# Second expert mixture scatters its results; feature attention spreads VectorE's small operations and takes four strips at once in its last units

## What is computed

```python
def _moe(x, Wg, W1, W3, W2):                      # layer 5, HIDDEN = 704, TOP_K = 2
    gate_weights = jax.nn.softmax(jnp.einsum('bsd,de->bse', x, Wg), axis=-1)
    topk_w, topk_idx = jax.lax.top_k(gate_weights, TOP_K)
    topk_w = topk_w / jnp.sum(topk_w, axis=-1, keepdims=True)
    ...
        y = jnp.einsum('bsh,hd->bsd', jax.nn.silu(x @ W1[e]) * (x @ W3[e]), W2[e])
        out = out + combine[..., e:e + 1] * y

def _L3_xattn_ref(q, k, v):                       # layer 6: b = 16, d = 64, m = n = 256
    qh = q.reshape(b * 8, 8, m); kh = k.reshape(b * 8, 8, n); vh = v.reshape(b * 8, 8, n)
    sm = jax.nn.softmax(jnp.einsum('bdm,bdn->bmn', qh, kh) / sqrt(8), axis=-1)
    ret = jnp.einsum('bmn,bcn->bcm', sm, vh)
```

## Time and profile before

| | us |
|---|---|
| median of three runs (lowest, highest) | 1216.42 (1215.36, 1218.13) |
| the profiled execution, its own time | 1219.71 |
| its span, first to last instruction | 1217.9 |
| busy in the span: PE, DVE, ACT, POOL | 1068.7, 577.4, 370.0, 258.0 |
| second mixture, first gather of tokens to last addition to X | 658.57 to 884.97 |
| feature attention, first score matmul to last addition to X | 888.52 to 1065.50 |

### The profile page before, as it was taken

The page is one execution under the profiler, slowest core; times in us unless marked ns, Lnnn a source line. Parts: engine busy times, 40 slices in busy tenths (PEclk is TensorE's granted clock), DMA queues, the critical chain, the costliest instruction groups (busy, mean ns, idle before and its releaser), DMA issues.

```text
span 1217.9 us, 18073 instructions
## 1 busy us (share of the span) xinstructions
PE 1068.7 (88%) x6946; PEld 713.4 (59%) x6946; DVE 577.4 (47%) x1304; ACT 370.0 (30%) x691; POOL 258.0 (21%) x332
## 2 busy tenths in 40 slices
PE   5877999979999999978774999999179999889989
PEld 4665578746767677667663777777133333243457
DVE  6976412244343343355474221221266777248692
ACT  3641123232221221204210222221015555526560
POOL 4212332420000000003521111100452433011350
PEclk9995989989999999989986999999659999978999
DMA  9002023211010010065043102110230000010000
GB/s 269 24 2 95 17 71 86 79 31 49 18 36 28 25 36 5 10 211 216 2 168 109 31 27 104 35 35 18 74 148 1 1 1 1 1 69 1 0 9 26
DMA packets 36059, 66.11 MB, mean 54 GB/s; under 512 B 4456, under 2 KB 26824, under 8 KB 34440
## 3 DMA queue, kind: packets, MB, share of 16 engines
q1 hardware_dynamic: 25608, 48.70, 11.9%
q0 software_dynamic: 3744, 10.23, 3.1%
q10 hardware_dynamic: 6624, 6.03, 1.4%
HBM read 54.72 MB, written 10.22 MB: 53 GB/s over the span
## 4 chain that ended last, share of the span: by engine, by line
PE 74%; DVE 17%; issue 3%; ACT 3%; DMA 2%; POOL 2%; SPq 0%; DVEq 0%; ACTq 0%
PE bank L344 22%; PE bank L1132 12%; PE bank L1156 7%; PE bank L1413 5%; PE bank L2069 4%; PE bank L2087 3%; PE bank L1423 3%; PE bank L2108 3%; PE bank L2497 2%; PE bank L1145 2%; DVE big L1959 2%; PE bank L1398 2%; PE bank L1388 1%; PE bank L2121 1%; PE bank L2503 1%
## 5 line engine op out<-in xcount | busy, mean ns | idle before, releaser
L1132 PE MATMUL bank<-big 128*128 x552 | 155.5, 426 | 3.6 <-ACT big L1006 1.7
L344 PE MATMUL bank<-XNT,big 128*128 128x512 f32 x296 | 143.4, 636 | 4.5 <-DVE big L2246 2.8
L1132 PEld LDWEIGHTS bank<-big 128*128 128x128 f32 x552 | 98.0, 194 | 50.5 <-issue 12.1
L2069 PE MATMUL bank<-big,xs 32*128 32x512 f32 x256 | 94.2, 781 | 36.5 <-DVE xs L271 30.5
L265 POOL TENSOR_TENSOR rstd<-ve,half 128x1 f32<-128x1 f32 x64 | 38.7, 605 | 366.9 <-DVE ve L259 366.5
L1959 DVE TENSOR_REDUCE big<-bank 128x2 f32<-128x512 f32 x128 | 81.9, 685 | 39.6 <-PE bank L2069 39.2
L344 PEld LDWEIGHTS bank<-XNT,big 128*128 128x128 f32 x296 | 57.9, 203 | 72.1 <-issue 64.0
L1156 PE MATMUL bank<-big 128*128 (+1 forms) x368 | 87.2, 380 | 1.1 <-ACT big L1021 1.1
L2021 ACT ACTIVATE big<-bank 128x1024 f32<-128x1024 f32 x64 | 65.5, 1024 | 52.4 <-PE bank L2087 52.3
L950 DVE TENSOR_TENSOR big<-big,bank 128x704 f32<-128x704 f32 x23 | 20.4, 889 | 124.7 <-ACT big L1014 124.7
L2087 PE MATMUL bank<-big 32*128 32x512 f32 x256 | 78.3, 690 | 0.2
(11 more groups left out here) (344 smaller groups left out, 1785.5 us busy)
## 6 DMA issues: line engine op xcount, KB each, us to landing
big<-m_gu SPq DMA_DIRECT2D x8, 1408.0 KB
big<-a_qkv SPq DMA_DIRECT2D x16, 384.0 KB, 3.5
big<-m_d SPq DMA_DIRECT2D x8, 768.0 KB
yg<-big ACTq DMA_DIRECT2D x46, 128.0 KB
big<-m_gu SPq DMA_DIRECT2D x8, 352.0 KB
big<-a_o SPq DMA_DIRECT2D x16, 128.0 KB, 2.1
big<-f_keys SPq DMA_DIRECT2D x1, 2048.0 KB, 9.2
big<-p_gu SPq DMA_DIRECT2D x1, 2048.0 KB, 7.8
```

Source lines behind the costliest of these rows:

```text
L344: ins = e.matmul(out, a, b, start=start and n == 0, stop=stop and n == len(pairs) - 1)
L1132: ins = e.matmul(out, xgT[s % 2][:, kb, :], WB[:, bass.ds(at[s] + (kb * 2 * F + c * chunk), chunk)], start=kb == 0, stop=kb == KB - 1)
L2069: e.matmul(bank[:, step_bank(step), :], k.xs[t % 2][q, b * P:(b + 1) * P], cm[t % 2][q, 2 * jp:2 * jp + 2].rearrange("p j n -> p (j n)"), ...
```

## The change

The second mixture. The index that each slot carries is now the place of its result in `yg`: 128 + 1024 times the choice + the token (`token_at`, one more index table, so `CONST` is 13), and 0 for padding. `xn` is stored twice, with 128 rows of padding ahead, so that the same index gathers the tokens. Each result tile is scattered by POOL with an indirect DMA (`deliver`), where ScalarE's queue stored it. The two results of a token then lie at fixed rows, and SP loads them with plain DMAs, one per row tile into four buffers (`sp_last`, which `program` issues after the next layer's `sp_first`). The first mixture keeps its way.

Feature attention. 5 units (`FRONT`) instead of 6 stand ahead of the first transposed strips, and two follow them in the first round. VectorE's list is cut in halves: two maxima, one small operation, two maxima, one small operation; the reciprocal is two halves of 128 columns. From unit 26 (`LAST`) on, where no scores are left, the transposed strips use three pairs of banks in turn, both pairs are issued one after the other, then both value products of the unit before; the turned maxima and the sorted result move to bank 6.

```diff
@@ -780,19 +784,27 @@
     xg, ya = ring[:, 0:RING], ring[:, RING:2 * RING]
+    pairs = ring.rearrange("p (n q) d -> p n q d", q=2)
     gw = k.gates[:, shared_expert * 1]
     g = k.dram
-    xn_d, yg_d = g["xn"], g["yg"]
+    if shared_expert:
+        xn_d, yg_d = g["xn"][0:T], g["yg"]
+    else:
+        xn_d, yg_d = g["xn"], g["yg"][0:2 * T + P]
+        to_xn = xn_d[P:].rearrange("(c t p) d -> t p c d", p=P, t=NT)
+        from_yg = yg_d[P:].rearrange("(c t p) d -> t p c d", p=P, t=NT)
     if k.moe_at is None:
...
     S, start = k.moe, dict(k.moe_at)
-    ends = dict(gate_ld=16 * (1 + 4 * shared_expert), wts=16 * 2 * E, xn_st=16 * NT, lg_ps=NT, mx=1, ex=1, mk=1, cnt=1,
+    ends = dict(gate_ld=16 * (1 + 4 * shared_expert), wts=16 * 2 * E, xn_st=16 * (NT + 1 - LAG), lg_ps=NT, mx=1, ex=1, mk=1, cnt=1,
                 hot=2, inv_ps=1, inv_sb=1, inv_t=1, inv=1, eid=1, xgt_ps=TILES, xgt_sb=TILES, gu_ps=TILES, hs=TILES, h_sb=TILES,
-                ht_ps=TILES, ht_act=TILES, ht_dve=TILES * (NB > 4), y_ps=TILES, y_sb=TILES, ga0=16 * NT, ga1=16 * NT,
+                ht_ps=TILES, ht_act=TILES, ht_dve=TILES * (NB > 4), y_ps=TILES, y_sb=TILES, ga0=16 * NT * LAG, ga1=16 * NT * LAG,
                 sh_ps=6, sh_s=6, sh_u=6, sh_h=6, shy_ps=NT, shy=NT)
     ends.update({f"xg{q}": 16 * len(range(q, TILES, RING)) for q in range(RING)})
-    ends.update({f"y_st{q}": 16 * len(range(q, TILES, YS)) for q in range(YS)})
+    for q in range(YS):
+        ends[f"y_st{q}"], ends[f"dv{q}"] = [16 * len(range(q, TILES, YS)) * here for here in (LAG, 1 - LAG)]
+    ends.update({f"back{n}": 32 * (1 - LAG) for n in range(4)})
     k.moe_at = {n: start[n] + ends[n] for n in MOE_SEMS}
@@ -827,7 +839,20 @@
             e.wait_ge(k.ln_out, at0 + t + 1)
-            tell(e.dma_start(xn_d[t * P:(t + 1) * P, :], XN[:, t]), "xn_st", 16)
+            if shared_expert:
+                tell(e.dma_start(xn_d[t * P:(t + 1) * P, :], XN[:, t]), "xn_st", 16)
+            else:
+                tell(e.dma_start(to_xn[t], bc(XN[:, t], 1, 2)), "xn_st", 16)
+                if t == 0:
+                    tell(e.dma_start(xn_d[0:P], XN[:, 0]), "xn_st", 16)
+    def sp_last(e):
+        for q in range(YS):
+            after(e, f"dv{q}", ends[f"dv{q}"])
+        for t in range(NT):
+            if t >= 4:
+                e.wait_ge(k.x_tile, done0 + t - 3)
+            tell(e.dma_start(pairs[:, t % 4], from_yg[t]), f"back{t % 4}", 16)
@@ -837,13 +862,31 @@
                 tell(e.tensor_tensor(both, both, sg[n % 2][0:FB[n % 3]], ALU.mult), "sh_h")
-        after(e, "inv", 1)
-        after(e, "xn_st", 16 * NT)
-        for s in range(TILES):
+        def fetch(s):
             if s >= RING:
...
                  f"xg{s % RING}", 16)
+        def deliver(s):
+            after(e, "y_sb", s + 1)
+            if s >= 1:
+                after(e, f"dv{(s - 1) % YS}", 16 * ((s - 1) // YS + 1))
+            tell(e.indirect_dma_start(yg_d, bass.IndirectOffsetOnAxis(ap=inv[:, s:s + 1], axis=0), ys[s % YS], None),
+                 f"dv{s % YS}", 16)
+        after(e, "inv", 1)
+        after(e, "xn_st", ends["xn_st"])
+        for s in range(RING):
+            fetch(s)
+        for s in range(TILES):
+            if s + RING < TILES:
+                fetch(s + RING)
+            if not shared_expert:
+                deliver(s)
+        if not shared_expert:
+            return
         for q in range(YS):
@@ -959,7 +1003,7 @@
             if s >= YS:
-                after(e, f"y_st{s % YS}", 16 * (s // YS))
+                after(e, f"y_st{s % YS}" if LAG else f"dv{s % YS}", 16 * (s // YS))
             tell(e.tensor_copy(ys[s % YS], k.bank[:, Y[s % 2], 0:D]), "y_sb")
@@ -971,10 +1015,14 @@
         for t in range(NT):
-            p = t % 2
-            after(e, f"ga{p}", 32 * (t // 2 + 1))
-            ch.step(e.scalar_tensor_tensor(k.X[:, t], ya[:, 2 * p], wA[:, t:t + 1], k.X[:, t], ALU.mult, ALU.add))
-            e.scalar_tensor_tensor(k.X[:, t], ya[:, 2 * p + 1], wB[:, t:t + 1], k.X[:, t], ALU.mult, ALU.add)\
+            if shared_expert:
+                both = ya[:, 2 * (t % 2):2 * (t % 2) + 2]
+                after(e, f"ga{t % 2}", 32 * (t // 2 + 1))
+            else:
+                both = pairs[:, t % 4]
+                after(e, f"back{t % 4}", 16 * (t // 4 + 1))
+            ch.step(e.scalar_tensor_tensor(k.X[:, t], both[:, 0], wA[:, t:t + 1], k.X[:, t], ALU.mult, ALU.add))
+            e.scalar_tensor_tensor(k.X[:, t], both[:, 1], wB[:, t:t + 1], k.X[:, t], ALU.mult, ALU.add)\
                 .then_inc(k.x_tile, 1)
@@ -1036,10 +1084,10 @@
                 rows(s + 1)
-            if s >= 1 + LAG:
-                store(s - 1 - LAG)
-        for s in range(TILES - 1, TILES):
-            store(s)
+            if LAG and s >= 2:
+                store(s - 2)
+        if LAG:
+            store(TILES - 1)
@@ -1837,7 +1886,8 @@
     NU = UNITS * NT
-    AHEAD = UNITS + 2
+    AHEAD, FRONT = UNITS + 2, UNITS + 1
+    LAST = NU - AHEAD
     STEPS = 4
@@ -1874,10 +1924,29 @@
+    def units_ahead(u):
+        return [n for n in ((FRONT, AHEAD) if u == 0 else (u + AHEAD,)) if n < NU]
+    def pair_banks(u, pair):
+        if u < LAST:
+            return TB + strips(pair)[0]
+        return (4, 2, 0)[(2 * (u - LAST) + (pair == A_)) % 3]
+    def maxima_bank(t):
+        return spare_bank(UNITS * t - 2, NTB)
+    def result_bank(t):
+        return spare_bank(UNITS * (t + 1) + 1, OB)
+    def spare_bank(u, b):
+        return b if u < LAST else SBK + SBN - 1
     def strips(pair):
...
-    def sp(e):
+    def sp_first(e):
         e.wait_ge(k.moe["y_ps"], k.moe_at["y_ps"] - TILES + NT)
@@ -1960,37 +2029,47 @@
+        def inverse(t, half):
+            after(e, "od", t + 1)
+            c = slice(half * P, (half + 1) * P)
+            ch.step(e.reciprocal(rec[:, c], od[:, D + half * P:D + (half + 1) * P]))
         def quotient(t):
-            after(e, "od", t + 1)
-            ch.step(e.reciprocal(rec, od[:, D:2 * D]))
             e.tensor_tensor(tmp, od[:, 0:D], rec, ALU.mult).then_inc(S["v_sb"], 1)
...
             e.tensor_tensor(k.X[:, t, :], k.X[:, t, :], tmp, ALU.add).then_inc(k.x_tile, 1)
+        def rest(u, half):
+            t, n = divmod(u, UNITS)
+            if n == 0 and half == 0 and t + 2 < NT:
+                ln_stats_dve(e, k, ch, t + 2, t % 2)
+            if n == 1 and half == 0 and t + 2 < NT:
+                norm(t + 2)
+            if n == 2 and t > 0:
+                inverse(t - 1, half)
+            if n == 3 and t > 0:
+                quotient(t - 1) if half == 0 else final(t - 1)
...
         ln_stats_dve(e, k, ch, 1, 1)
-        for u in range(AHEAD):
+        for u in range(FRONT):
             for r in range(RG):
...
         for u in range(NU):
-            t = u // UNITS
-            if u + AHEAD < NU:
-                for r in range(RG):
-                    top(u + AHEAD, r)
-            if u % UNITS == 0 and t + 2 < NT:
-                ln_stats_dve(e, k, ch, t + 2, t % 2)
-            if u % UNITS == 1 and t + 2 < NT:
-                norm(t + 2)
-            if u % UNITS == 2 and t > 0:
-                quotient(t - 1)
-            if u % UNITS == 3 and t > 0:
-                final(t - 1)
+            ahead = [(n, r) for n in units_ahead(u) for r in range(RG)]
+            for half in (0, 1):
+                for n, r in ahead[half * len(ahead) // 2:(half + 1) * len(ahead) // 2]:
+                    top(n, r)
+                rest(u, half)
+        inverse(NT - 1, 0)
+        inverse(NT - 1, 1)
         quotient(NT - 1)
@@ -2017,8 +2096,8 @@
                     after(e, "v_ps", u - 1)
-                r = slice(strips(pair)[0], strips(pair)[1] + 1)
-                e.activation(pt[u % 2][:, r].rearrange("p r j n -> p r (j n)"), k.bank[:, r, :], ACT.Exp,
+                r, b = slice(strips(pair)[0], strips(pair)[1] + 1), pair_banks(u, pair)
+                e.activation(pt[u % 2][:, r].rearrange("p r j n -> p r (j n)"), k.bank[:, b:b + 2, :], ACT.Exp,
                              scale=float(G) ** -0.5).then_inc(S["ex"], 1)
@@ -2076,24 +2155,31 @@
                 after(e, "less", 2 * t + 2)
-            if u % UNITS == 3 and pair == B_ and t + 1 < NT:
-                after(e, "nm", t + 2)
-            if u % UNITS == 2 and t > 0 and pair == B_:
-                after(e, "od", t)
-            if u > 0:
-                after(e, "ex", 2 * u - (1 if pair == B_ else 0))
+            if u < LAST:
+                if u % UNITS == 3 and pair == B_ and t + 1 < NT:
+                    after(e, "nm", t + 2)
+                if u % UNITS == 2 and t > 0 and pair == B_:
+                    after(e, "od", t)
+                if u > 0:
+                    after(e, "ex", 2 * u - (pair == B_))
+            else:
+                after(e, "ex", 2 * u - 2 + (pair == A_))
+                if u == LAST and pair == B_:
+                    after(e, "mx", STEPS * NU)
+                if u == LAST and t > 0:
```

(36 more changed lines are left out.)

25 lines of the change are left out of this document (15 added, 10 removed).

## The result

The changed kernel took 1184.65 us (median of four, 1182.83 to 1184.73), the kernel before beside it 1216.62; the ratio is 0.974, 95% interval 0.9718 to 0.9762, a gain of 32.0 us where 24.4 were forecast. In a later run the changed kernel took 1183.30 beside 1215.22, 0.9733 (0.9712 to 0.9753).

What follows compares the result with a forecast made beforehand. Taken as bounds: POOL, DMA and VectorE in a chain at the second mixture's end, TensorE with VectorE stalls in the row tiles. 10.5 + 8.5 + 0.8 + 4.8 - 0.15 = 24.4 us off 1216.42 gave 1192.0; range 1185 to 1204.

Steps and rivals of the forecast that it cites:

- The mixture's end: Second mixture, last result copy to last update of X: scatter and pair loads replace sixteen gathers, 10.5 us saved, 6 to 12.
- What I costed at nothing in the mixture: 23 further scatters on POOL, normalised tokens stored twice and one more index table: expected to be covered, no cost.
- The row tiles: Five feature-attention tiles: spreading VectorE's small operations removes a 1.2 us stall of PE; 8.5 us saved, 3 to 12.
- My walk: Stepping through one row tile with traced durations: the next unit starts 0.5 to 1.4 us earlier, 1.1 taken.
- The start: Feature attention's start: about one unit's transposed work slips into gaps between scores, 0.8 us saved, 0 to 1.5.
- The last units: Last six units of feature attention, four strips at once: 17.9 us against 22.74, 4.8 saved, 2 to 6.5.
- The last reciprocal: End of feature attention: the last reciprocal in two halves costs 0.15 us.
- Slow padding: Rival, second mixture: padding rows written to one row take up to 8 us per tile; 1196.5 us, chance 0.12.
- Serial writes: Rival, second mixture: writes to one row are serial, gain gone above 13.5 us a scatter, 1236 at 20; chance 0.05.
- VectorE stays the bound: Rival, row tiles: port waits refill the stall and the clock falls; 1 us saved instead of 8.5, 1199.5; chance 0.15.
- Four strips without gain: Rival, last six units: hand-overs to ACT and POOL fill the time; 1.5 us saved, 1195.3; chance 0.05.
- They will not all fall together: Reason for the range: low bounds of all terms save 11 us (1205.4), high ones 32 (1184.4), not expected all at once.

Runs made afterwards that it cites:

- the direct undoing: The changed kernel with VectorE's small operations put back behind all four maxima of a unit: 1199.91 us, ratio 0.9872.

## Why the prediction was wrong, point by point

**The mixture's end: right.** 10.5 us forecast. The kernels with the old end took 25.35, 25.65 and 25.49, those with the new one and the single padding row 14.12 to 14.78, mean 14.4: 11.1 saved. Every step of the chain was within 0.4 us.

**What I costed at nothing in the mixture: right.** From the first gather to the last result copy both kernels took 201.05 us. What came 4.9 us earlier was chance: the kernel with unchanged mixtures and the one with only the table were early too, by 6.9 and 7.0.

**The row tiles: the term that was mis-sized.** I wrote "I take 1.1: 17.65 us per tile", which gave 8.5. The mechanism was right, the size was not: five tiles gave 13.7 us, by the mean of three traces of the old order. Three things are in the 5.2 us between them. First the tile, 2.5 us in five: 17.20 measured, 16.93 in the last. My walk let product and addition take 1.3 each in the worse case, and I took a value between that and the better one; they took 0.49 and 0.41, and no idle gap of PE was left. 17.65 is what the uncut reciprocal gives. Second, the sum itself, 0.6 us: 97.4 - 88.3 is 9.1, and I kept 8.5 as an allowance for falls of the clock; there were none, not even with the 0.44 us more per tile of the uncut reciprocal. Third, the base, 2.1 us: I took the 97.41 of one execution as what the old order costs. It holds a tile of 18.75 and one of 17.94 beside three of 20.0 to 20.3. The three traces of the old order and the one that brings it back read 97.4, 99.7, 101.35 and 101.36, the six of the new one 85.8 each. On the mean of the three it is 13.7 saved, not 8.5; the direct undoing cost 15.3 us by medians. My high bound of 12 was "no stall left" in that one trace, so it could not hold it.

I also read the tile of 17.94 wrongly. I wrote that the product took 0.42 us away from POOL's addition ("0.42 elsewhere"). In the trace of before POOL's addition stands beside that product too:

```profile
1003.51 1.53 POOL L1905 TENSOR_TENSOR big<-big 128x512 f32<-128x512 f32 x1 [8.66 <-ACT big L2011]
```

The product began 0.02 us ahead of it, at 1003.49, and here it was POOL's operation that was long, 1.53 us instead of 1.27.

**The start: not shown.** 0.8 forecast, nothing by the medians; it is under what a run can tell.

**The last units: right.** 4.8 forecast, 5.0 in every trace.

**The last reciprocal: right.** 0.15 forecast, 0.2 measured.

With the measured terms the sum is 11.1 + 13.7 + 5.0 - 0.2 = 29.6 of the 32.0, inside the interval of the first verdict (29.0 to 34.3). The remaining 2.4 are not attributed: the medians of unprofiled executions have no stages. They may be no more than what a comparison on one chip can be off by: the two kernels with spread padding and with six units ahead, whose times are the changed kernel's, gained only 29.8 us on theirs (1184.36 against 1214.17).

**The rivals.** Slow padding was real in its mechanism, at a sixth of its price: 0.7 us, not the 4.5 by which the rival's time lay above the forecast; the forecast had 0.8 us for it. The Trainium skill (DMA: Bandwidth & Descriptors, rules for kernel authors) lets every write of a repeated index go out; the equal packet counts agree. Serial writes are refuted: they needed 13.5 us a scatter, and the last one had landed within 3.14. VectorE stays the bound is refuted in the change, but its mechanism, a VectorE operation that lasts until POOL's is over, appeared as soon as an experiment moved an operation: 1.70, 2.13 and 2.19 us for what takes 0.4 to 0.5. The rule of SBUF — State Buffer in the Trainium skill (the two separate sides), one instruction at a time and the first to start keeps the port, agrees with those of 1.70 and 2.13. In the one of 2.19 VectorE's record begins 0.02 us ahead of POOL's and it is VectorE's that is long; in the old tile of 17.94 it began just as much ahead and POOL's was long. So at that distance the starts of the records do not tell who waits. The change's order happens to miss most of POOL's work. Four strips without gain is refuted.

**The range** was too narrow on its fast side because the bounds of its largest uncertain term were drawn from one execution. "They will not all fall together" was true of the small terms; this one lay beyond its bound. But the measured terms alone, 29.6 us, give 1187.0, inside the range: it took the 2.4 us without a stage as well to bring the result 0.35 us below it. What failed for sure is the term, and not the edge.

## What to carry to other kernels

A stall of an engine that feeds TensorE is priced twice, by its length and by the clock that may fall behind it, and the second part differs from one execution to the next: take it from several tiles in several traces, and let the high bound hold every tile at its worst. Work on a feeding engine that is short of its partner by little is better spread between the pieces the partner waits for than kept together: place is worth more than size. When a stage is bound by TensorE alone, the slack of the others is where a neighbouring stage's serial work can go.
